# Window-attention scores on sixteen 32x32 tiles of the array, with their transposes in the shared ring of PSUM banks

## The chip, the cores and the metric
The kernel runs on one core of a Trainium2 chip. The time is what the device takes for one execution, in microseconds. "Before" is the median of three runs.

## What is computed
The input is x of shape (32, 256, 128). Four stages follow, each of the form x = x + f(layernorm(x)), cut here to what matters:

```python
# stage W: window attention, 16 heads of 8, keys and values shared by 8 heads each (KV = 2)
q = (x @ Wq + bq); k = (x @ Wk + bk); v = (x @ Wv + bv)      # 128, 16 and 16 columns
# blocks of 32 queries see 64 padded keys, u in [t, t + 32)
scores = where(win_mask, einsum('bhntd,bhnud->bhntu', qb, kb), -inf)
out = einsum('bhntu,bhnud->bhntd', softmax(scores), vb) @ Wo + bo
# stage F: h = x @ W_exp + b_exp; butterfly; gelu; butterfly; @ W_con + b_con
# stage L: linear attention, phi = elu + 1; out = q (k^T v) / (q sum(k)); @ Wproj + bproj
# stage G: the feed-forward stage again
```

## The kernel before, in words
The 8192 tokens are cut into 16 groups of 512 (four tiles of 128 tokens). A group passes through the stages P (norm, queries, keys, values), W (window attention), F (feed-forward), L (linear attention) and G (feed-forward again). The butterflies are folded at the start into two plain matrices, w1b and w2.

The kernel is a software pipeline written out by hand. Each engine runs its own list of work once per turn t (`turn`, one per engine), and each item works on group t - lag; the lags run from 0 to 6. The order of TensorE's items is the table PRODUCTS (lines 40 to 49): name, lag and PSUM bank. The lists of VectorE, ScalarE, GpSimdE and SyncE stand in their own `turn` functions and in VECTOR, PHI, POOL_STEPS, NORMED, BIASED and TRANSFERS. An engine works its list strictly in order. All waits are counts on semaphores: `product` counts finished products of TensorE, and `drained_b` counts how often bank b was emptied. `free(g, name)` (line 393) makes a product wait until the item before it on the same bank has been drained.

PSUM has eight banks of 512 fp32 columns. Before, ps_s has two (bank "S", the scores), ps_t has two (bank "T", the transposed scores), and four are the ring, "0" to "3", shared by 31 of the 39 products of a turn.

Names used below, with their lines: `P.kv` (508) and `P.q` (514) are the keys and values, and the queries. `W.S0` to `W.S3` (`scores`, 412) are the scores of tile j: first a bf16 product of the mask (422), then the fp32 product of queries and keys (427). `shift_by_max` (811) takes the row maximum and subtracts it (VectorE). `W.T0` to `W.T3` (438) are eight 128x128 transposes per tile; `probs_out` (674) takes the exp of them on ScalarE into probs_t. `W.PV0` to `W.PV3` (446) multiply with the values, `head_outputs` (823) divides by the sum. `W.V` (433) transposes the spread values. `W.oT`, `L.oT` and the four `.xT` (401) are four transposes each, copied out by ScalarE (`copy_out`, 659). `F.up0` to `F.up3`, `G.up0` to `G.up3` (461) are the up products, each followed by a gelu on ScalarE (665) into hid; `F.down`, `G.down` (468) use all four. `L.q`, `L.k0`, `L.k1`, `L.kv`, `L.out0`, `L.out1`, `L.proj` belong to linear attention. ScalarE alternates between exp and gelu, and each change of the function puts an ACT_TABLE_LOAD ahead of the ACTIVATE, at the ACTIVATE's line.

The scores need every head's keys in the partitions of its queries. `spread_keys` (283) copies the 8 rows of keys of each of the two key heads to the partitions of its eight query heads, one DMA per query head, sixteen a group, into a block-diagonal tensor kx, whose other entries are zero. A score matmul is then 64 rows (8 heads of 8) by 32 queries, with 8 heads x 64 keys = 512 columns; four blocks of 32 queries times two halves make eight matmuls on eight 64x32 tiles of the array.

```python
for c in range(4):
    for a in range(KV):
        half = slice(HPK * HD * a, HPK * HD * (a + 1))
        last = nc.tensor.matmul(
            ps_s[32 * c:32 * c + 32, a], q_t[half, P * j + 32 * c:P * j + 32 * c + 32],
            kx[half, :, TSPAN * j + 32 * c:TSPAN * j + 32 * c + SPAN], ...)
```

Of the kernel before, what the change touches and what calls it, by code (L numbers as in the profile page):

```python
# [7 lines left out]
F32 = mybir.dt.float32  # L8
BF16 = mybir.dt.bfloat16
# [8 lines left out]
WIN = 32  # L18
# [13 lines left out]
KVW = DIM + HEADS  # L32
LN_EPS = 1e-5
# [22 lines left out]
]  # L56
PHI = [("L.q", 3), ("L.k0", 3), ("L.k1", 3)]
POOL_STEPS = [
    ("L.rv", 5), ("L.rstd", 5), ("L.nm", 5), ("L.nmr", 5),
    ("F.rv", 3), ("F.rstd", 3), ("F.nm", 3), ("F.nmr", 3),  # L60
    ("W.rv", 2), ("W.rstd", 2), ("W.nm", 2), ("W.nmr", 2),
    ("P.rv", 0), ("P.rstd", 0), ("P.nm", 0), ("P.nmr", 0),
]
NORMED = [("L.xn", 5), ("F.xn", 3), ("W.xn", 2), ("P.xn", 0)]
BIASED = [("L.xb", 5), ("P.xb", 1), ("F.xb", 3), ("W.xb", 2)]
TRANSFERS = {"P.v": 2, "P.kx": 1, "P.x": 0, "G.y": 6}
TURNS = NG + 6
# [35 lines left out]
def window_and_linear_attention_with_butterfly_ffn(  # L103
    nc, x, wq, bq, wk, bk, wv, bv, wo, bo, wqkv_t, wproj_t, bproj, w_exp_t, up_m, up_c, up_b,
    down_m, down_c, w_con, b_con, down_b, ident_c, spread_c, kvmask_c, band_c, vones_c, out,
):
    with ExitStack() as ctx:
# [12 lines left out]
        bandb = sb("bandb", [P, HPK, SPAN], BF16)  # L120
        half = sb("half", [P, TILES])
        wq_s = sb("wq_s", [P, P])
        wkv_s = sb("wkv_s", [P, 2 * KV * HD])
# [4 lines left out]
        bkv_s = sb("bkv_s", [2 * KV * HD, 1])  # L128
# [31 lines left out]
        kv_t = sb("kv_t", [2 * KV * HD, TILES, TSPAN])  # L160
        kx = sb("kx", [P, HPK, TILES * TSPAN])
# [23 lines left out]
        ps_s = ctx.enter_context(nc.psum_tensor("ps_s", [P, 2, 512], F32))  # L185
        ps_t = ctx.enter_context(nc.psum_tensor("ps_t", [P, HPK, P], F32))
        ring = [ctx.enter_context(nc.psum_tensor(f"ring{i}", [P, 512], F32)) for i in range(4)]

        def bank(name):
# [23 lines left out]
                   for b in "ST0123"}  # L213
# [7 lines left out]
        kx_in = Count(sem("kx_in"), [("P.kx", TRANSFERS["P.kx"])], 16 * HEADS)  # L221
# [29 lines left out]
        def _(sp):  # L251
            consts = [(ident, ident_c), (spread, spread_c), (kvmask, kvmask_c), (band, band_c)]
            for dst, src in consts:
# [4 lines left out]
                (wq_s[:], wq), (wkv_s[:, 0:KV * HD], wk), (wkv_s[:, KV * HD:], wv), (bq_s[:], column(bq)),  # L258
                (bkv_s[0:KV * HD, :], column(bk)), (bkv_s[KV * HD:, :], column(bv)), (wo_s[:], wo),
# [35 lines left out]
            def spread_values(g):  # L295
# [4 lines left out]
                for c in range(4):  # L300
                    for kv in range(KV):
                        r = KV * HD + kv * HD
# [8 lines left out]
            def turn(t):  # L311
                for g in due(t, 2):
                    spread_values(g)
                for g in due(t, 1):
                    spread_keys(g)
                for g in due(t, 0):
                    load_x(g)
                for g in due(t, 6):
                    store_y(g)
# [7 lines left out]
        def _(pool):  # L327
# [41 lines left out]
            def turn(t):  # L369
                for g in due(t, 5):  # L370
                    normalise(g, "L")
                for g in due(t, 3):
                    normalise(g, "F")
# [6 lines left out]
                for g in due(t, 3):  # L380
                    add_bias(g, "F", bproj_s, "F.down", "L.proj")
                for g in due(t, 0):
                    normalise(g, "P")
                for g in due(t, 2):
                    add_bias(g, "W", bffn_s, "W.proj", "F.down")
# [6 lines left out]
        def _(pe):  # L392
# [19 lines left out]
            def scores(g, j):  # L412
# [623 lines left out]
```

## Time and profile before
| what | before |
|---|---|
| runs | 678.38, 679.83, 678.49 us; median 678.49 |
| profiled execution, own time | 678.38 us |
| span of the profile, first to last instruction | 676.6 us |
| instructions | 14602 |
| mean granted TensorE clock | 0.985 of 2.4 GHz |
| VectorE, ScalarE, GpSimdE busy | 419.6, 427.1, 308.8 us |

In rows of a timeline the first number is the start in us from the first instruction, the second the time until the last of the merged instructions ends, "x" their number. The ends of matmuls are modelled and overlap the next start, so the cost of a step is read from start to start. An fp32 matmul leaves two records. A bracket tells of idle time before a row, and who ended it.

### The profile page before, as it was taken

What the parts mean: (1) busy time and instruction counts of PE and PEld (TensorE: products, weight loads), DVE (VectorE), ACT (ScalarE), POOL (GpSimd) and SP (SyncE); (2) the same over time, 40 slices, a digit from 0 to 9 for tenths busy, and PEclk for the clock granted to TensorE, in tenths of its full rate; (3) what the DMA queues carried; (4) which work ended last, traced back from release to release, by engine and by line L of the source; (5) the groups of instructions that cost most, each with busy time, mean ns of one, the idle gap of its engine ahead of it and who ended that gap; (6) DMA issues with size and microseconds to landing.
All of it is one profiled execution on the core that took longest, in us unless ns stands there. A gap on an engine that the chain in (4) does not pass through costs nothing.

```text
span 676.6 us, 14602 instructions
## 1 busy us (share of the span) xinstructions
PE 623.5 (92%) x5140; PEld 409.5 (61%) x5140; DVE 419.6 (62%) x1114; ACT 427.1 (63%) x585; POOL 308.8 (46%) x585
## 2 busy tenths in 40 slices
PE   0847698999999999999999999999999999999986
PEld 0633354656575766757585757667575857575855
DVE  2356556677767666676667676666766676674340
ACT  0302275666868768685868687686858686868341
POOL 6002408164645354654546453546545464446332
PEclk9977899999999999999999999999999999999999
DMA  5500101101011110101111111101001111000001
GB/s 164 190 16 9 33 13 29 21 20 22 21 21 36 18 39 12 42 8 19 33 21 37 21 36 19 39 13 42 9 19 32 22 36 34 8 1 16 16 17 31
DMA packets 31671, 20.96 MB, mean 31 GB/s; under 512 B 9328, under 2 KB 27504, under 8 KB 31600
## 3 DMA queue, kind: packets, MB, share of 16 engines
q1 hardware_dynamic: 31600, 20.03, 12.1%
q8 instruction: 42, 0.69, 0.4%
q14 instruction: 29, 0.24, 0.1%
HBM read 9.53 MB, written 4.19 MB: 20 GB/s over the span
## 4 chain that ended last, share of the span: by engine, by line
PE 88%; DVE 5%; ACT 3%; issue 2%; SPq 1%; DMA 1%; POOL 0%; DVEq 0%; ACTq 0%
PE ring L475 18%; PE ring L465 17%; PE ps_t L443 8%; PE ring L403 8%; PE ps_s L427 8%; PE ring L452 5%; PE ring L484 4%; PE ring L500 4%; PE ps_s L422 3%; PE ring L508 2%; PE ring L535 2%; PE ring L524 2%; PE ring L514 2%; PE ring L491 2%; PE ps_t L562 1%
## 5 line engine op out<-in xcount | busy, mean ns | idle before, releaser
L814 DVE TENSOR_REDUCE rowmax<-ps_s 128x16 f32<-128x1024 f32 x64 | 78.0, 1219 | 39.6 <-PE ps_s L427 39.5
L679 ACT ACTIVATE probs_t<-ps_t 128x1024 f32<-128x1024 f32 x64 | 65.5, 1023 | 29.5 <-PE ps_t L443 29.0
L819 DVE TENSOR_TENSOR shifted<-ps_s,rowmax 128x1024 f32<-128x1024 f32 x64 | 78.4, 1225 | 7.0 <-PE ps_t L443 0.5
L671 ACT ACT_TABLE_LOAD x57 | 73.1, 1283 | 8.7 <-PE ring L465 7.9
L443 PE MATMUL ps_t<-ident,shifted 128*128 128x128 f32 x512 | 68.7, 278 | 3.3 <-DVE shifted L819 3.3
L679 ACT ACT_TABLE_LOAD x42 | 53.9, 1283 | 26.2 <-PE ps_t L443 26.2
L427 PE MATMUL ps_s<-kx,q_t 64*32 64x512 f32 x1024 | 70.2, 618 | 0.0
L465 PE MATMUL ring<-xT_G,w1b 128*128 128x512 f32 x128 | 67.4, 613 | 2.3 <-ACT xT_G L663 1.0
L443 PEld LDWEIGHTS ps_t<-ident,shifted 128*128 128x128 f32 x512 | 58.5, 143 | 12.6 <-issue 9.1
L475 PEld LDWEIGHTS ring<-w,hid_G 128*128 128x128 f32 x512 | 58.4, 192 | 9.5 <-issue 4.9
L475 PE MATMUL ring<-w,hid_G 128*128 128x128 f32 x512 | 61.2, 278 | 2.8 <-ACT hid_G L671 2.8
L475 PE MATMUL ring<-w,hid_F 128*128 128x128 f32 x512 | 60.9, 277 | 0.6 <-issue 0.2
L475 PEld LDWEIGHTS ring<-w,hid_F 128*128 128x128 f32 x512 | 58.4, 192 | 4.3 <-issue 4.3
L465 PE MATMUL ring<-xT_F,w1b 128*128 128x512 f32 x128 | 60.3, 595 | 0.4 <-ACT xT_F L663 0.4
L671 ACT ACTIVATE hid_G<-ring,b 128x512 f32<-128x512 f32 x64 | 43.9, 687 | 20.5 <-PE ring L465 20.0
L364 POOL TENSOR_TENSOR xb_P<-x_P,bo_s 128x512 f32<-128x512 f32 x16 | 20.5, 1282 | 73.5 <-DVE x_W L806 70.1
L338 POOL TENSOR_SCALAR rv_F<-mv_F 128x4 f32<-128x4 f32 x16 | 3.6, 226 | 96.5 <-DVE mv_F L792 96.5
L828 DVE STREAM_TRANSPOSE o_raw<-ring 128x256 f32<-128x256 f32 x64 | 28.2, 440 | 25.3 <-PE ring L452 25.2
L806 DVE TENSOR_TENSOR x_G<-ring,xb_L 128x512 f32<-128x512 f32 x16 | 11.1, 692 | 49.0 <-PE ring L475 49.0
L338 POOL TENSOR_SCALAR rv_L<-mv_L 128x4 f32<-128x4 f32 x16 | 3.6, 226 | 81.7 <-DVE mv_L L792 81.7
L671 ACT ACTIVATE hid_F<-ring,b 128x512 f32<-128x512 f32 x64 | 40.3, 688 | 0.4 <-PE ring L465 0.2
L452 PE MATMUL ring<-probs_t,vx 128*32 128x256 f32 x512 | 37.6, 388 | 0.0
(120 smaller groups left out, 1205.6 us busy)
## 6 DMA issues: line engine op xcount, KB each, us to landing
kx<-kv_t SPq DMA_DIRECT2D x256, 20.0 KB
x_P<-in_x SPq DMA_DIRECT2D x16, 256.0 KB, 2.9
out_x<-x_G SPq DMA_DIRECT2D x16, 256.0 KB, 3.2
vx_t<-kv_t SPq DMA_DIRECT2D x128, 8.0 KB
up_s<-in_up_m SPq DMA_DIRECT2D x7, 256.0 KB, 5.6
down_s<-in_down_m SPq DMA_DIRECT2D x7, 256.0 KB, 5.6
u_t<-in_w_exp_t SPq DMA_DIRECT2D x1, 258.0 KB, 3.7
vx_t<-in_vones_c SPq DMA_DIRECT2D x1, 256.0 KB, 2.9
```

Of the source, the lines that this page charges most:

```text
L403: last = nc.tensor.transpose(bank(name)[:, P * j:P * (j + 1)], src[:, j], ident[:])
L427: last = nc.tensor.matmul(ps_s[32 * c:32 * c + 32, a], q_t[half, P * j + 32 * c:P * j + 32 * c + 32], kx[half, :, TSPAN * j + 32 * c:TSPAN ...
L443: last = nc.tensor.transpose(ps_t[:, h], shifted[:, j % 2, h].rearrange("p k u -> p (k u)"), ident[:])
L452: last = nc.tensor.matmul(bank(name)[32 * c:32 * c + 32, 0:HPK * 32], vx[:, j, c], probs_t[:, j % 2, :, 32 * c:32 * c + 32], start=True, s ...
L465: nc.tensor.matmul(bank(name)[:], w1b[:, P * c:P * (c + 1)], x_t[s][:], start=True, stop=True).then_inc(product.sem, 1)
L475: last = nc.tensor.matmul(bank(name)[:, P * j:P * (j + 1)], hid[s][:, c, P * j:P * (j + 1)], w2[:, c], start=(c == 0), stop=(c == CH - 1))
L484: last = nc.tensor.matmul(bank(f"{s}.proj")[:, P * j:P * (j + 1)], src[:, P * j:P * (j + 1)], weights[:], start=True, stop=True)
L671: nc.scalar.activation(hid[s][:, c], bank(name)[:], ACT.Gelu, bias=b1[:, c:c + 1]).then_inc(drained[BANK[name]].sem, 1)
L679: nc.scalar.activation(probs_t[:, j % 2], ps_t[:], ACT.Exp).then_inc(drained["T"].sem, 1)
L814: nc.vector.tensor_reduce(rowmax[:, j], s, AX_X, ALU.max).then_inc(vec.sem, 1)
L819: nc.vector.tensor_tensor(shifted[:, j % 2].rearrange("p h k u -> p k h u"), ps_s[:].rearrange("p k (h u) -> p k h u", u=SPAN), m, ALU.sub ...
L828: nc.vector.transpose(o_raw[:, j % 2].rearrange("p h r -> p (h r)"), bank(name)[:, 0:HPK * 32]).then_inc(own.sem, 1)
```

## The change
The scores run on sixteen 32x32 tiles: a matmul has 32 rows (4 heads of 8), 32 queries and 4 heads x 64 keys = 256 columns; row strip r writes the first 256 columns of bank r of ps_s, which now has four banks. The order of the query columns is changed on the host (`query_order`), so that a strip holds heads of both key heads in turn. The weights of the keys are repeated four times (`key_rows`), so that P.kv gives 64 rows of keys and 16 of values, and `spread_keys` needs four DMAs of 32 rows each instead of sixteen of 8. ps_t is gone: the eight transposes of a tile are two products, W.Tja and W.Tjb, of four transposes each, in banks of the ring, and each half is drained by its own exp. At the start, the butterflies' down product uses a bank of ps_s. All lists have a new order, lags and banks; TensorE's lags now run from 0 to 5, and the scores of tiles 0 and 1 are made in the turn of their keys.

```diff
 PRODUCTS = [
+    ("W.S2", 1, "S"), ("G.up2", 5, "3"), ("G.up0", 5, "1"), ("W.PV0", 1, "0"), ("F.xT", 2, "2"),
+    ("W.T1b", 1, "3"), ("L.k1", 3, "1"), ("L.k0", 3, "0"), ("W.PV1", 1, "3"), ("F.up2", 2, "2"),
+    ("W.S3", 1, "S"), ("P.xT", 0, "1"), ("F.up1", 2, "3"), ("F.up0", 2, "0"), ("G.up1", 5, "2"),
+    ("L.kv", 3, "1"), ("W.T2b", 1, "2"), ("P.kv", 0, "3"), ("W.T2a", 1, "0"), ("W.T3a", 1, "1"),
+    ("W.T3b", 1, "2"), ("L.out1", 3, "3"), ("W.PV2", 1, "0"), ("F.up3", 2, "1"), ("W.PV3", 1, "2"),
+    ("P.q", 0, "3"), ("F.down", 2, "1"), ("L.out0", 3, "0"), ("W.S0", 0, "S"), ("W.oT", 1, "3"),
+    ("G.down", 5, "2"), ("G.xT", 4, "3"), ("W.proj", 1, "1"), ("L.oT", 3, "0"), ("G.up3", 4, "2"),
+    ("W.S1", 0, "S"), ("L.xT", 2, "0"), ("W.T0b", 0, "1"), ("W.T0a", 0, "3"), ("L.q", 2, "2"),
+    ("L.proj", 3, "0"), ("W.V", 0, "3"), ("W.T1a", 0, "1"),
 ]
...
-                for h in range(HEADS):
-                    kv = h // HPK
-                    sp.dma_start(kx[h * HD:(h + 1) * HD, h % HPK],
-                                 kv_t[kv * HD:(kv + 1) * HD].rearrange("d j n -> d (j n)")).then_inc(kx_in.sem, 16)
+                for h in range(RH):
+                    kv = h % KV
+                    sp.dma_start(kx[h:P:RH, h], kv_t[kv * ROWS * HD:(kv + 1) * ROWS * HD].rearrange("d j n -> d (j n)")
+                                 ).then_inc(kx_in.sem, 16)
...
-                    for a in range(KV):
-                        half = slice(HPK * HD * a, HPK * HD * (a + 1))
+                    for r in range(ROWS):
+                        rows = slice(32 * r, 32 * r + 32)
                         last = nc.tensor.matmul(
-                            ps_s[32 * c:32 * c + 32, a], q_t[half, P * j + 32 * c:P * j + 32 * c + 32],
-                            kx[half, :, TSPAN * j + 32 * c:TSPAN * j + 32 * c + SPAN],
+                            ps_s[32 * c:32 * c + 32, r, 0:RH * SPAN], q_t[rows, P * j + 32 * c:P * j + 32 * c + 32],
+                            kx[rows, :, TSPAN * j + 32 * c:TSPAN * j + 32 * c + SPAN],
...
-            def probs_transposed(g, j):
+            def probs_transposed(g, j, part):
-                for h in range(HPK):
-                    last = nc.tensor.transpose(ps_t[:, h], shifted[:, j % 2, h].rearrange("p k u -> p (k u)"), ident[:])
+                for i, h in enumerate(PAIRS[part]):
+                    last = nc.tensor.transpose(bank(name)[:, P * i:P * (i + 1)],
+                                               shifted[:, j % 2, h].rearrange("p k u -> p (k u)"), ident[:])
...
-                nc.scalar.activation(probs_t[:, j % 2], ps_t[:], ACT.Exp).then_inc(drained["T"].sem, 1)
+                nc.scalar.activation(probs_t[:, j % 2, PAIRS[part][0]:PAIRS[part][-1] + 1].rearrange("p h t -> p (h t)"),
+                                     bank(name)[:], ACT.Exp).then_inc(drained[BANK[name]].sem, 1)
```

ScalarE's new list per turn, lags in brackets: copy L.xT (3), exp T0a and T0b (1), phi of L.q (3), exp T1a (1), gelu G2 and G0 (5), exp T1b (1), copy F.xT (2), phi and copies of L.k1 and L.k0 (3), gelu F2 (2), copy P.xT (0), gelu F1 and F0 (2), gelu G1 (5), exp T2b (1), drain P.kv (0), exp T2a, T3a and T3b (1), gelu F3 (2), drain P.q (0), copies of W.oT (1), G.xT (4) and L.oT (3), gelu G3 (4). The lists of VectorE, GpSimdE and SyncE are reordered in the same way. The groups of a turn of ScalarE and of TensorE may be numbered with lags that differ by one where the work crosses the end of a turn.

## Rows read from the trace of the kernel before

**Rows 1.** The page, part 1: busy time, share of the span and instructions.
```profile
PE 623.5 (92%) x5140; PEld 409.5 (61%) x5140; DVE 419.6 (62%) x1114; ACT 427.1 (63%) x585; POOL 308.8 (46%) x585
```

**Rows 2.** Timeline of TensorE, P.kv of groups 1, 4, 8 and 15.
```profile
59.92 1.04 PE L508 MATMUL ring<-xT_P,wkv_s 128*32 128x512 f32 x2
...
153.05 1.04 PE L508 MATMUL ring<-xT_P,wkv_s 128*32 128x512 f32 x2
...
298.08 1.04 PE L508 MATMUL ring<-xT_P,wkv_s 128*32 128x512 f32 x2
...
558.25 1.04 PE L508 MATMUL ring<-xT_P,wkv_s 128*32 128x512 f32 x2
```

**Rows 3.** Timeline of TensorE inside one full turn.
```profile
308.54 3.84 PE L475 MATMUL ring<-w,hid_G 128*128 128x128 f32 x32
312.21 1.02 PE L514 MATMUL ring<-xT_P,wq_s 128*128 128x512 f32 x2
313.17 0.64 PE L452 MATMUL ring<-probs_t,vx 128*32 128x256 f32 x8
313.74 0.76 PE L535 MATMUL ring<-kvs,phi_q 128*128 128x144 f32 x4
314.33 0.60 PE L403 MATMUL ring<-ident,xn_L 128*128 128x128 f32 x4
314.77 0.66 PE L535 MATMUL ring<-kvs,phi_q 128*128 128x144 f32 x4
...
316.71 1.06 PE L484 MATMUL ring<-wo_s,o_wt 128*128 128x128 f32 x8
...
334.68 0.60 PE L403 MATMUL ring<-ident,vx_t 128*128 128x128 f32 x4
335.21 1.04 PE L508 MATMUL ring<-xT_P,wkv_s 128*32 128x512 f32 x2
336.19 0.41 PE L422 MATMUL ps_s<-bandb,spreadb 64*32 64x512 bf16 x8
336.41 1.04 PE L427 MATMUL ps_s<-kx,q_t 64*32 64x512 f32 x16
337.38 1.07 PE L452 MATMUL ring<-probs_t,vx 128*32 128x256 f32 x16
```

**Rows 4.** Timeline of ScalarE inside the same turn.
```profile
315.96 0.60 ACT L663 ACTIVATE o_wt<-ring 128x512 f32<-128x512 f32 x1 [0.33 <-PE ring L403]
...
318.25 0.69 ACT L671 ACTIVATE hid_G<-ring,b 128x512 f32<-128x512 f32 x1
318.83 0.59 ACT L663 ACTIVATE xT_L<-ring 128x512 f32<-128x512 f32 x1
319.31 0.60 ACT L663 ACTIVATE o_lt<-ring 128x512 f32<-128x512 f32 x1
...
324.29 0.36 ACT L698 ACTIVATE v_ext<-ring 128x256 f32<-128x256 f32 x1
...
325.29 0.37 ACT L698 ACTIVATE v_ext<-ring 128x256 f32<-128x256 f32 x1
...
333.20 1.28 ACT L679 ACT_TABLE_LOAD   x1 [0.26 <-PE ps_t L443]
334.50 1.02 ACT L679 ACTIVATE probs_t<-ps_t 128x1024 f32<-128x1024 f32 x1
...
336.37 0.87 ACT L708 ACTIVATE kv_t<-ring,bkv_s 32x288 f32<-32x288 f32 x2 [0.85 <-PE ring L508]
...
338.56 0.69 ACT L671 ACTIVATE hid_F<-ring,b 128x512 f32<-128x512 f32 x1
```

**Rows 5.** The page, part 5, groups: busy, mean ns of one, idle before.
```profile
L814 DVE TENSOR_REDUCE rowmax<-ps_s 128x16 f32<-128x1024 f32 x64 | 78.0, 1219 | 39.6 <-PE ps_s L427 39.5
...
L679 ACT ACT_TABLE_LOAD x42 | 53.9, 1283 | 26.2 <-PE ps_t L443 26.2
```

**Rows 6.** Timeline of SyncE's queue: four of the sixteen key transfers.
```profile
337.63 2.69 SPq L292 DMA_DIRECT2D kx<-kv_t  x4
```

More of the change, by code:

```diff
@@ L32 @@
 KVW = DIM + HEADS
+ROWS = 4
+RH = HEADS // ROWS
+KROWS = KV * ROWS * HD
+KVROWS = KROWS + KV * HD
 LN_EPS = 1e-5
@@ L369, in turn @@
             def turn(t):
-                for g in due(t, 5):
-                    normalise(g, "L")
+                for g in due(t, 4):
+                    add_bias(g, "F", bproj_s, "F.down", "L.proj")
                 for g in due(t, 3):
+                    add_bias(g, "W", bffn_s, "W.proj", "F.down")
                     normalise(g, "F")
@@ L507, in attention_kv @@
                 free(g, "P.kv")
-                nc.tensor.matmul(bank("P.kv")[0:2 * KV * HD, :], wkv_s[:], x_t["P"][:], start=True, stop=True
+                nc.tensor.matmul(bank("P.kv")[0:KVROWS, :], wkv_s[:], x_t["P"][:], start=True, stop=True
                                  ).then_inc(product.sem, 1)
@@ L561, in butterflies @@
                     for c in range(CH):
-                        last = nc.tensor.matmul(ps_t[:, c], down_s[m][:, c], d_t[n % 2][:, c],
+                        last = nc.tensor.matmul(ps_s[:, 2, P * c:P * (c + 1)], down_s[m][:, c], d_t[n % 2][:, c],
                                                 start=True, stop=True)
@@ L573, in turn @@
             def turn(t):
-                for g in due(t, 2):
+                for g in due(t, 1):
+                    scores(g, 2)
+                for g in due(t, 5):
+                    ffn_up(g, "G", 2)
+                    ffn_up(g, "G", 0)
+                for g in due(t, 1):
+                    weighted_values(g, 0)
+                for g in due(t, 2):
+                    norm_transposed(g, "F", "W")
+                for g in due(t, 1):
+                    probs_transposed(g, 1, "b")
+                for g in due(t, 3):
+                    linear_kv_rows(g, 1)
+                    linear_kv_rows(g, 0)
+                for g in due(t, 1):
+                    weighted_values(g, 1)
+                for g in due(t, 2):
+                    ffn_up(g, "F", 2)
+                for g in due(t, 1):
+                    scores(g, 3)
+                for g in due(t, 0):
+                    norm_transposed(g, "P", "P")
+                for g in due(t, 2):
+                    ffn_up(g, "F", 1)
+                    ffn_up(g, "F", 0)
+                for g in due(t, 5):
+                    ffn_up(g, "G", 1)
+                for g in due(t, 3):
+                    linear_state(g)
+                for g in due(t, 1):
+                    probs_transposed(g, 2, "b")
+                for g in due(t, 0):
+                    attention_kv(g)
+                for g in due(t, 1):
+                    probs_transposed(g, 2, "a")
+                    probs_transposed(g, 3, "a")
+                    probs_transposed(g, 3, "b")
+                for g in due(t, 3):
+                    linear_out(g, 1)
+                for g in due(t, 1):
                     weighted_values(g, 2)
-                for g in due(t, 6):
-                    ffn_down(g, "G")
+                for g in due(t, 2):
+                    ffn_up(g, "F", 3)
                 for g in due(t, 1):
+                    weighted_values(g, 3)
+                for g in due(t, 0):
                     attention_q(g)
@@ L582, in turn @@
                 for g in due(t, 2):
-                    weighted_values(g, 3)
-                for g in due(t, 4):
+                    ffn_down(g, "F")
+                for g in due(t, 3):
                     linear_out(g, 0)
-                for g in due(t, 5):
-                    norm_transposed(g, "G", "L")
-                for g in due(t, 4):
-                    linear_out(g, 1)
-                for g in due(t, 2):
+                for g in due(t, 0):
+                    scores(g, 0)
@@ L637, in turn @@
[L637 to L647 removed]
+                    norm_transposed(g, "L", "F")
+                for g in due(t, 0):
+                    probs_transposed(g, 0, "b")
+                    probs_transposed(g, 0, "a")
@@ L903, in turn @@
             def turn(t):
+                for g in due(t, 3):
+                    residual(g, "F", "F.down", "W")
+                    moments(g, "F")
                 for g in due(t, 4):
-                    linear_normalised(g, 1)
+                    linear_normalised(g, 0)
+                for g in due(t, 1):
+                    shift_by_max(g, 0)
+                for g in due(t, 6):
+                    residual(g, "G", "G.down", "L")
                 for g in due(t, 2):
@@ L919, in turn @@
                         butterflies()
+                for g in due(t, 1):
+                    head_outputs(g, 0)
+                    shift_by_max(g, 2)
                 for g in due(t, 3):
```

270 lines of the change are left out of this document (118 added, 152 removed), and 16 rows, old and new, of tables (PRODUCTS, VECTOR).

## The prediction
> **What bounds the kernel now.** First I read the page's busy times: TensorE is busy 623.5 of 676.6 us [rows 1]. The starts of one product that occurs once a turn, the keys and values of a group (P.kv), then give the rhythm [rows 2]: 59.92 for group 1, 153.05 for group 4, 298.08 for group 8 and 558.25 for group 15. With the next start, 335.21 [rows 3], a full turn is 37.13 us, and a turn of the filling pipeline about 31. The timeline of TensorE inside a turn shows step after step without an idle bracket [rows 3], so the bound is TensorE's own list of work. The timeline of ScalarE shows something else [rows 4]: the load of an activation table (1.28 us) begins only after the product that its ACTIVATE waits for is done; the row at 333.20 has 0.26 us of idle time before it, ended by PE, and the group of these loads has 26.2 us of idle time, all ended by the transposes [rows 5]. Today this delay holds nobody up: the transposes have ps_t for themselves and return to it a quarter of a turn later.
>
> **What the change does to TensorE's work.** Steps are distances between starts. Four transposes take 0.44 (314.33 to 314.77), a 512-column product 0.96 less 0.09 = 0.87, PV 0.57, a down product 3.67, two state products with the entry into another array shape 0.59 [rows 3]. That entry costs 0.09: the values' transposes take 0.53 where 32-column work follows, 0.44 elsewhere.
> Scores: the masks take 0.22 (336.19 to 336.41), the scores 0.97 (to 337.38), together 1.19 per tile, four per turn [rows 3]. The eight matmuls of 64x32 run side by side, for 0.22 is one 512-column pass. Sixteen 32x32 ones of 256 columns would halve the passes (0.11 + 0.43) if they ran side by side too. The way out of the shape (0.11, 1.19 less 0.22 and 0.86) stays, and sixteen instead of eight weight loads must fit under shorter passes, for which I add 0.1. So 0.75. No row shows a 32x32 tile; the bounds are 0.65 (all overlapped) and 1.19 (no gain), and nothing excludes more than 1.19. I take a value near the low end, since half as many columns per tile is the same kind of work as the row before.
> In a sentence by itself: the Trainium skill, TensorE: Matmul & The Clock Gate, section "Wait — 56ns, not 53.3ns?", states a floor of about 25 ns between the starts of matmuls however narrow, and by it 48 of them would take 1.2 us and the gain would be nil; whether that holds across separate tiles, the rows of this kernel decide (rival B).
> The rest of the work: PV0 and PV1 lose their neighbourhood with a score step, which adds two entries and 0.1 of exit (+0.3); P.kv widens from 32 to 80 columns and so is no longer a narrow tile (-0.1). TensorE's work per turn goes from 37.1 to 37.1 - 4x0.44 + 0.2 = 35.6; adding up the steps of the new order gives 35.0; I take 35.3.
>
> **What it adds: waits for banks.** The transposes of the probabilities now come in eight halves and take turns with everything else on four ring banks: 39 products a turn in place of 31. Who must drain a bank before the next product starts is read off the new list. Where that drain begins with a table load, the way from the end of a product to the next start on its bank is: 0.30 until ScalarE starts (P.kv ends at 335.21 + 0.87, its drain starts at 336.37), 1.30 for the load (333.20 to 334.50), the ACTIVATE, and 0.15 back (o_wt ends at 316.56, the product that needs it starts at 316.71) [rows 3, 4]. A half's exp has no row; a copy of the same 512 columns takes 0.60, and between two that follow each other 0.48; gelu takes 0.69, or 0.58 in a row; the three steps of k 1.00 per half; kv's two 0.87 [rows 4]. The two halves cost ScalarE about what the whole did (0.48 + 0.60 against 1.02). The new order has six loads in a turn, the old one eight.
> Going once around a full turn, from the start of the values' transposes (V):
> 1. V to end of G.up2: T1a waits for the exp of T0b (0.48), then T1a 0.44 + 0.09, S2 0.75, G.up2 0.87: 2.63.
> 2. G.up2 to T1b (bank 3): 0.30 + 1.30 + 0.69 + 0.15 = 2.44. TensorE has 1.97 of work to put there. Then T1b 0.44.
> 3. T1b to T2b: ScalarE without a gap does load, exp, copy of F.xT, k1, k0, load, gelu F2, copy of P.xT, F1, F0, G1: 0.30+1.30+0.48+0.48+2.00+0.10+1.30+0.58+0.48+0.58+0.58+0.69+0.15 = 9.02; TensorE has 8.1 there. Then T2b 0.44.
> 4. T2b to PV2 (T2b's exp, kv's drain, T2a's exp): 0.30+1.30+0.48+0.87+0.60+0.15 = 3.70 against 2.8. Then PV2 0.57 and F.up3 0.87.
> 5. F.up3 to F.down: 2.44 against 1.5.
> 6. F.down to the end of T0a, TensorE alone: 3.67+0.59+0.75 (S0)+0.44+3.67+0.44+0.87+0.44+0.96+0.75 (S1)+0.44+0.88 = 13.90.
> 7. T0a to V (bank 3): 0.30+1.30+0.60+0.15 = 2.35 against 1.7.
> Sum 2.63+2.44+0.44+9.02+0.44+3.70+1.44+2.44+13.90+2.35 = **38.8 us**, against 37.13 now. S3 lies in stretch 3, under ScalarE, so its gain is worth nothing; three score steps count. With 0.65 for them the loop is 38.5, with 1.19 it is 40.1.
> On the loads trace and skill differ: here one costs 1.30 with what lies around it [rows 4]. The Trainium skill, ScalarE: Activation LUTs, section "What ACT_TABLE_LOAD costs", gives 1283 ns and adds a drain of some 1380 ns; by that the five loads of the loop would add 6.9 us to it. The trace has the 1.28 and not the drain.
> Other engines: VectorE's reductions and subtractions keep 1024 elements a partition, 1.22 us each [rows 5]; S2 to S3 leave it more than 7 us for 2.5. GpSimdE's list only changes its order. SyncE issues four key transfers a group in place of sixteen, at 0.67 each (2.69 for four) [rows 6]. In full turns nobody waits for keys: P.kv to S0 leaves 9 us. If a transfer four times as large landed later by as much, S0 would wait; I count nothing and keep up to 1 us a turn for the range.
>
> **The sum.** Up to P.kv of group 1 nothing changes (59.9). The three turns from there to group 4 take 93.1 now; they are bound by latency, of which twelve issues of 0.67 = 8 us go, fully in the first and less as work fills the turns, and fewer table loads are in them. Between 69 and 93 I take 80. Then one turn without the down product of G, 38.8 - 3.7 = 35, and ten full turns, 388: P.kv of group 15 at 563. From there to the end it is 118.3 now; the last group has the same stages before it, at five lags instead of six, and the chains of each stage (moments, normalising, transposing, gelu) stay; between 113 and 125 I take 120. Span 683, with the 1.8 us that lie around the span in the profiled execution (678.38 against 676.6) 685. The profiled execution is 0.1 us under the median of the three, 678.49.
>
> **Rivals.**
> A, *TensorE stays the bound.* If the table loads ran while TensorE still worked on the product (or the waits overlapped otherwise), stretches 2 to 5 and 7 shrink below TensorE's work and a turn is 35.3: 59.9 + 80 + 32 + 353 + 118 + 1.8 = 645. For it: TensorE has no idle bracket in a full turn today [rows 3]. Against it: every load on the timeline comes after its product. It decides once the waits sum to under 1.8 us a turn; by the walk they sum to 3.8. Chance 0.16.
> A', *half of it*: chains shorter by 0.2 to 0.3 each, a turn of 36 to 37.8, 655 to 677. Chance 0.16.
> B, *the sixteen tiles don't run together*: the score step stays at 1.19, a turn is 40.1 and the fill a little longer: 685 + 11x1.3 + 2 = 701. Chance 0.10.
> C, *keys late*: one wait of 1 us per turn at S0: 696. Chance 0.06.
>
> **The numbers.** The forecast, the loop of 38 to 39.6, has 0.52: 677 to 694. Most of it is slower; 0.2% (1.4 us) is what a measurement of this kernel can tell. Faster: A, A' less a little, and some of the forecast, 0.31. Same 0.07. Slower 0.62. The range leaves out most of A and the far side of B: 656 to 703.
>
> **What would show it.** P.kv to P.kv in the full turns near 38.8; TensorE's busy share down to about 90% there; waits of F.down on hid_F near 0.9, of T1b on hid_G 0.5, of V on probs_t 0.6 and of T2b on hid_G, each once a turn; the score step 0.75, the sixteen masks starting together; six loads a turn; 0.44 for each half's transposes. The forecast is wrong if TensorE has no waits in the full turns (A), or if the score step is above 1 us (B).

## The result and the profile after

| | before | after |
|---|---|---|
| median of the runs (4 each, same chip) | 679.16 us (678.38 to 680.63) | 726.85 us (723.81 to 727.71) |
| span of the profile | 676.6 us | 722.0 us |
| P.kv of group 1 starts at | 59.9 | 63.4 |
| P.kv 1 to P.kv 4 | 93.1 | 92.1 |
| P.kv 4 to P.kv 15 | 405.2 | 434.9 |
| P.kv 15 to the end | 118.3 | 131.6 |
| one full turn | 37.13 | 39.73 |
| table loads in the whole run | 114 | 92 |

The ratio is 1.069, with a 95% interval of 1.065 to 1.073. The kernel became slower, as forecast, but by 48 us and not by 6.5, and 726.85 is above the upper end of the range (703). The two profiled executions differ by 45.4 us of span: 29.7 us of it, two thirds, lie between P.kv 4 and P.kv 15, in the full turns, and 13.3 us behind the last P.kv.

First the page of the changed kernel: busy times [rows 1], chain of waits by engine, and the groups that answer to [rows 5].

```profile
PE 632.7 (88%) x6676; PEld 423.5 (59%) x6676; DVE 420.1 (58%) x1114; ACT 398.8 (55%) x627; POOL 305.8 (42%) x585
...
PE 72%; ACT 12%; DVE 8%; issue 6%; SPq 1%; DMA 1%; POOL 0%; ACTq 0%; DVEq 0%; POOLq 0%
...
L832 DVE TENSOR_REDUCE rowmax<-ps_s 128x16 f32<-128x1024 f32 x64 | 77.9, 1217 | 7.2 <-PE ps_s L429 6.3
L682 ACT ACT_TABLE_LOAD x46 | 59.0, 1283 | 34.3 <-PE ring L469 34.0
...
L690 ACT ACT_TABLE_LOAD x41 | 52.6, 1283 | 19.3 <-PE ring L445 19.3
```

ScalarE is less busy than before (398.8 against 427.1 us): 22 loads of 1.28 us are gone, which is 28.2 of these 28.3. TensorE's share of the span falls from 92 to 88%, and its share of the chain that ended last from 88% (the same line of the page before) to 72%. The load groups say where to look: 34.0 us of idle time ahead of gelu's loads end with an up product, 19.3 us ahead of exp's loads with a transpose. The reduction costs what it did (1217 ns), so VectorE's own work isn't the matter.

TensorE's P.kv of groups 1, 4 and 15, which answer to [rows 2]:

```profile
63.40 1.08 PE L512 MATMUL ring<-xT_P,wkv_s 128*80 128x512 f32 x2
...
155.49 1.02 PE L512 MATMUL ring<-xT_P,wkv_s 128*80 128x512 f32 x2
...
590.40 1.02 PE L512 MATMUL ring<-xT_P,wkv_s 128*80 128x512 f32 x2
```

TensorE's timeline in one full turn (answers to [rows 3]; first the start, then the time until the last of the merged instructions ends):

```profile
311.68 0.63 PE L445 MATMUL ring<-ident,shifted 128*128 128x128 f32 x4
312.14 1.02 PE L512 MATMUL ring<-xT_P,wkv_s 128*80 128x512 f32 x2
313.00 1.04 PE L445 MATMUL ring<-ident,shifted 128*128 128x128 f32 x8
314.42 0.63 PE L445 MATMUL ring<-ident,shifted 128*128 128x128 f32 x4 [0.39 <-ACT probs_t L690]
...
315.86 0.64 PE L456 MATMUL ring<-probs_t,vx 128*32 128x256 f32 x8
316.42 1.13 PE L469 MATMUL ring<-xT_F,w1b 128*128 128x512 f32 x2
...
318.05 1.13 PE L518 MATMUL ring<-xT_P,wq_s 128*128 128x512 f32 x2
319.86 3.81 PE L479 MATMUL ring<-w,hid_F 128*128 128x128 f32 x32 [0.69 <-DVE o_raw L846]
...
336.45 0.63 PE L405 MATMUL ring<-ident,vx_t 128*128 128x128 f32 x4 [0.23 <-ACT probs_t L690]
...
337.50 0.33 PE L424 MATMUL ps_s<-bandb,spreadb 32*32 32x256 bf16 x16
337.62 0.91 PE L429 MATMUL ps_s<-kx,q_t 32*32 32x256 f32 x32
338.47 1.98 PE L469 MATMUL ring<-xT_G,w1b 128*128 128x512 f32 x4
...
341.80 0.63 PE L445 MATMUL ring<-ident,shifted 128*128 128x128 f32 x4 [0.20 <-ACT hid_G L682]
342.38 1.97 PE L504 MATMUL ring<-wl_s,xT_L 128*128 128x256 f32 x8
344.75 0.64 PE L456 MATMUL ring<-probs_t,vx 128*32 128x256 f32 x8 [0.41 <-ACT probs_t L690]
...
351.50 0.63 PE L445 MATMUL ring<-ident,shifted 128*128 128x128 f32 x4
```

Before, this view had no bracket in a full turn. Now there are five, all for drains that ScalarE does, together 1.92 us. The one of F.down at 319.86 names VectorE's o_raw, but F.down neither reads o_raw nor writes the bank that it empties. What it needs in the kernel are the gelus of the four up products, and the last of them, that of F.up3, also empties F.down's own bank. ScalarE's timeline shows it (it answers to [rows 4]):

```profile
317.63 1.28 ACT L682 ACT_TABLE_LOAD   x1 [1.13 <-PE ring L469]
318.93 0.69 ACT L682 ACTIVATE hid_F<-ring,b 128x512 f32<-128x512 f32 x1
...
334.42 1.28 ACT L690 ACT_TABLE_LOAD   x1 [0.26 <-PE ring L445]
335.71 1.09 ACT L690 ACTIVATE probs_t<-ring 128x512 f32<-128x512 f32 x2
...
339.67 1.28 ACT L682 ACT_TABLE_LOAD   x1 [1.24 <-PE ring L469]
...
342.51 1.28 ACT L690 ACT_TABLE_LOAD   x1 [0.28 <-PE ring L445]
```

F.up3 starts at 316.42 and ScalarE waits for it; only when it is done does the load begin (317.63), then the gelu (318.93 to 319.62), then F.down (319.86). ScalarE had stood idle for 1.13 us, in which most of the load would have fitted. This is the loop that the prediction walked.

### The profile page after: what moved, and what is told of

Its sections match the earlier page's. It is cut to its first block, busy times and chain, and to the rows that moved or that the text cites. A ratio compares the mean times of both kernels' runs of the same rounds, so it can differ in the third digit from the quotient of the medians.

```text
span 722.0 us, 17701 instructions
## 1 busy us (share of the span) xinstructions
PE 632.7 (88%) x6676; PEld 423.5 (59%) x6676; DVE 420.1 (58%) x1114; ACT 398.8 (55%) x627; POOL 305.8 (42%) x585
## 4 chain that ended last, share of the span: by engine, by line
PE 72%; ACT 12%; DVE 8%; issue 6%; SPq 1%; DMA 1%; POOL 0%; ACTq 0%; DVEq 0%; POOLq 0%
PE ring L479 16%; PE ring L469 14%; PE ring L405 7%; PE ring L445 7%; PE ps_s L429 6%; PE ring L456 4%; ACT probs_t L690 3%; PE ring L504 3%; PE ring L539 3%; PE ring L495 2%; PE ps_s L424 2%; ACT L682 2%; PE ring L512 2%; PE ring L528 2%; ACT hid_G L682 2%
## 5 line engine op out<-in xcount | busy, mean ns | idle before, releaser
L445 PE MATMUL ring<-ident,shifted 128*128 128x128 f32 x512 | 74.6, 280 | 10.6 <-ACT probs_t L690 7.2
L690 ACT ACTIVATE probs_t<-ring 128x512 f32<-128x512 f32 x128 | 70.7, 596 | 21.9 <-PE ring L445 21.4
L832 DVE TENSOR_REDUCE rowmax<-ps_s 128x16 f32<-128x1024 f32 x64 | 77.9, 1217 | 7.2 <-PE ps_s L429 6.3
L445 PEld LDWEIGHTS ring<-ident,shifted 128*128 128x128 f32 x512 | 58.1, 144 | 29.9 <-issue 25.5
L469 PE MATMUL ring<-xT_F,w1b 128*128 128x512 f32 x128 | 66.7, 624 | 0.1
L469 PE MATMUL ring<-xT_G,w1b 128*128 128x512 f32 x128 | 64.9, 613 | 1.8 <-ACT xT_G L674 1.4
L690 ACT ACT_TABLE_LOAD x41 | 52.6, 1283 | 19.3 <-PE ring L445 19.3
L479 PE MATMUL ring<-w,hid_G 128*128 128x128 f32 x512 | 59.9, 275 | 1.9 <-ACT hid_G L682 1.9
L429 PE MATMUL ps_s<-kx,q_t 32*32 32x256 f32 x2048 | 60.4, 394 | 0.0
L674 ACT ACTIVATE o_wt<-ring 128x512 f32<-128x512 f32 x16 | 9.6, 597 | 85.0 <-PE ring L405 85.0
L456 PE MATMUL ring<-probs_t,vx 128*32 128x256 f32 x512 | 40.9, 390 | 7.2 <-ACT probs_t L690 7.2
L682 ACT ACTIVATE hid_F<-ring,b 128x512 f32<-128x512 f32 x64 | 42.4, 690 | 3.8 <-PE ring L469 3.3
L824 DVE TENSOR_TENSOR x_F<-ring,xb_W 128x512 f32<-128x512 f32 x16 | 11.1, 692 | 56.1 <-PE ring L479 56.1
```

The lines of the kernel that those rows point to most:

```text
L429: last = nc.tensor.matmul(ps_s[32 * c:32 * c + 32, r, 0:RH * SPAN], q_t[rows, P * j + 32 * c:P * j + 32 * c + 32], kx[rows, :, TSPAN * j + ...
L445: last = nc.tensor.transpose(bank(name)[:, P * i:P * (i + 1)], shifted[:, j % 2, h].rearrange("p k u -> p (k u)"), ident[:])
L456: last = nc.tensor.matmul(bank(name)[32 * c:32 * c + 32, 0:HPK * 32], vx[:, j, c], probs_t[:, j % 2, :, 32 * c:32 * c + 32], start=True, s ...
L469: nc.tensor.matmul(bank(name)[:], w1b[:, P * c:P * (c + 1)], x_t[s][:], start=True, stop=True).then_inc(product.sem, 1)
L479: last = nc.tensor.matmul(bank(name)[:, P * j:P * (j + 1)], hid[s][:, c, P * j:P * (j + 1)], w2[:, c], start=(c == 0), stop=(c == CH - 1))
L682: nc.scalar.activation(hid[s][:, c], bank(name)[:], ACT.Gelu, bias=b1[:, c:c + 1]).then_inc(drained[BANK[name]].sem, 1)
```

## The experiments

**1. Are the waits the table loads?** Gelu is replaced by exp in both feed-forward stages, so that ScalarE never changes its table; what these stages compute is thus another function, of the same sizes, and a 512-column drain costs ScalarE 0.69 us with either. The same edit went into the kernel before.

```diff
-  nc.scalar.activation(hid[s][:, c], bank(name)[:], ACT.Gelu, bias=b1[:, c:c + 1]
+  nc.scalar.activation(hid[s][:, c], bank(name)[:], ACT.Exp, bias=b1[:, c:c + 1]
```

> The changed kernel with exp in place of gelu in both feed-forward stages, so that the function computed there is another one and ScalarE never changes its table. Theory L (the banks of the ring wait behind table loads): the 87 loads go, a full turn falls from 39.73 to TensorE's own work, 36.2 to 36.6 us, and the span from 722 to 670-685. Rival R (the ring is too full whatever the drains begin with): a turn stays above 38.5 us and the span above 705.

> The kernel before with the same replacement of gelu by exp. Both theories: a full turn is TensorE's work already, 37.13, and loses at most the 0.25 us wait of F.down: 36.8 to 37.1. Filling and draining lose a few loads on their chains: span 664 to 673. If a full turn falls by more than 0.5 us, loads were on the path of the old kernel too and the account of the change is wrong.

Measured, one execution each: the changed kernel 670.01 us, a full turn 36.49, from P.kv 15 to the end 118.3; the kernel before 671.19 us, 36.87 and 116.0. One load is left in each. So 91 loads less are worth 53.8 us of span in the changed kernel (722.0 to 668.2) and 113 less only 7.2 us in the one before (676.6 to 669.4). The price of a load is its place, not its number. And with the loads gone the changed kernel isn't slower: its turn is shorter by 0.38 us.

**2. The same functions, the loads earlier.** Exp alone proves too much (it takes the loads away, not their delay). So at six changes of the function a one-column ACTIVATE of the coming function on constant data stands ahead of the instruction that waits; the diff shows the one at F.up3. All loads and all of the computation stay.

```diff
+ def touch(func):
+     n = len(touched)
+     touched.append(func)
+     nc.scalar.activation(scratch[:, n:n + 1], bq_s[:], func)
...
  for g in due(t, 2):
+     touch(ACT.Gelu)
      gelu(g, "F", 3)
```

> The changed kernel; ScalarE gets a one-column ACTIVATE of the coming function ahead of the wait at each of the six changes of table in a turn, so that the load runs before the product is done; nothing else. Theory L: each wait behind a load shortens by up to 1.3 us where ScalarE is idle before it; full turn 36.3 to 37.0, time 675 to 692. Rival R: turn within 0.5 us of 39.73, time above 720.

> The kernel before with the same one-column ACTIVATEs ahead of its eight changes of table a turn. Full turns are TensorE's work: 36.9 to 37.15 us. Filling and draining have chains with loads on them (waits of 0.93 us of G.down on the last gelu): time 665 to 676 against 679. If the small ACTIVATEs themselves get in the way, 679 to 685.

Measured: the changed kernel 687.01 us, ratio to the kernel before 1.011 (1.010 to 1.013), with the same 92 loads and a turn of 36.96. The kernel before with the edit (eight changes a turn) 681.1 us, ratio 1.002 (1.001 to 1.003), turn 37.22. That is a little above what was expected: there was nothing to hide, and the small ACTIVATEs (0.20 us each) probably stand in the way, which no run shows apart. ScalarE's and TensorE's timelines of the changed kernel with early loads, at F.up3 and F.down:

```profile
302.18 1.28 ACT L747 ACT_TABLE_LOAD   x1
303.48 0.20 ACT L747 ACTIVATE scratch<-bq_s 128x1 f32<-128x1 f32 x1
303.59 0.67 ACT L683 ACTIVATE hid_F<-ring,b 128x512 f32<-128x512 f32 x1
```

```profile
302.08 1.12 PE L470 MATMUL ring<-xT_F,w1b 128*128 128x512 f32 x2
303.14 0.64 PE L457 MATMUL ring<-probs_t,vx 128*32 128x256 f32 x8
303.71 1.13 PE L519 MATMUL ring<-xT_P,wq_s 128*128 128x512 f32 x2
304.67 3.73 PE L480 MATMUL ring<-w,hid_F 128*128 128x128 f32 x32
```

The load now runs beside F.up3 (302.18 against 302.08), and F.down has no bracket. From start to start, both kernels: PV2 to F.down 4.00 before the edit and 3.15 with it, T2b to PV2 4.18 and 3.43, T1b to T2b 9.70 and 9.02, V to T1b 5.35 and 4.98, F.down to V 16.59 and 16.37. These five differences add up to 2.87 us, which is the difference of the two turns that were read (39.82 against 36.95). **The waits in the turn are the loads that begin only behind the product.**

**3. The score step.** It was predicted at 0.75 us and is 0.963 (337.50 to 338.47 in the timeline above): the masks 0.12, as expected, the scores 0.844 where 0.64 was counted. Looking at the score product in ever longer windows from its start shows how its 32 records begin:

```profile
337.62 0.40 PE L429 MATMUL ps_s<-kx,q_t 32*32 32x256 f32 x8
...
337.62 0.70 PE L429 MATMUL ps_s<-kx,q_t 32*32 32x256 f32 x24
```

Eight start before 337.70, sixteen more before 337.95, the last eight after that: three waves, where two full passes of sixteen would have done. Is that due to the order, in which the four strips of a block follow each other? The two loops were exchanged.

```diff
-  for c in range(4):
-      for r in range(ROWS):
-          rows = slice(32 * r, 32 * r + 32)
+  for r in range(ROWS):
+      rows = slice(32 * r, 32 * r + 32)
+      for c in range(4):
```

> The changed kernel with the sixteen masks and the sixteen score matmuls of a tile issued row strip by row strip instead of column block by column block; same work. In the changed kernel the 32 score records start in three waves (8, 16, 8) and the step is 0.96 us with the mask. Theory W (only eight weight loads run ahead, whatever their place): three waves again, 0.96. Theory S (weights for a strip whose matmuls are running have to wait, so strips should alternate late): two waves, step 0.75, a full turn 0.6 us shorter, span 715.

Measured, one execution: 725.21 us, turn 39.73, masks 0.12, scores 0.84 as before. The order of the tiles has no part in it. Why it is three waves (whether, say, no more than eight weights are loaded ahead) stays open; no run tested it further.

**4. What the narrower tiles and the four key transfers are worth.** The changed kernel got the scores of the kernel before back (eight 64x32 tiles of 512 columns), first with sixteen key transfers.

```diff
-  for r in range(ROWS):
-      rows = slice(32 * r, 32 * r + 32)
+  for r in range(2):
+      rows = slice(64 * r, 64 * r + 64)
...
-  for h in range(RH):
+  for r in range(ROWS):
+      for h in range(RH):
```

> The changed kernel with the score matmuls back on eight 64x32 tiles over two PSUM banks and the keys spread by sixteen transfers; order, halves and the four-bank ring are the changed kernel's. It prices the 32x32 tiles alone: the score step goes back from 0.96 to 1.20, three of the four count, so a full turn is 40.4 (39.73 + 0.7) and the span 732. Rival (the waits of ScalarE absorb all of it): 39.7 to 39.9, 724.

Measured, one execution: 821.47 us and a turn of some 46. That was no measure of the tiles. SyncE, TensorE and the windows around S0:

```profile
362.88 11.07 SPq L297 DMA_DIRECT2D kx<-kv_t  x16
```

```profile
375.43 0.63 PE L425 MATMUL ps_s<-bandb,spreadb 64*32 64x512 bf16 x8 [3.46 <-issue]
375.81 1.95 PE L430 MATMUL ps_s<-kx,q_t 64*32 64x512 f32 x16
377.69 1.11 PE L406 MATMUL ring<-ident,o_w 128*128 128x128 f32 x4
```

In the windows the columns are length, busy time of PE, PEld, DVE, ACT and POOL, granted clock, DMA share, GB/s.

```profile
371.90:375.40 3.50, 0.07 (x1) 0.00 (x1) 2.51 (x12) 0.00 (x0) 1.44 (x3) 0.83 0.17 29
375.40:381.00 5.60, 5.57 (x40) 3.76 (x41) 2.45 (x2) 0.60 (x1) 2.00 (x6) 0.50 0.09 16
```

Sixteen issues take 11 us, S0 of the same turn waits 3.46 us for the last keys, and the granted clock is 0.83 over this wait and 0.50 (its 1.2 GHz level) in the 5.6 us behind it, where masks and scores together take 2.26 us (375.43 to 377.69) in place of 1.20. So the repeated keys, which looked like a side matter of this change, are what allows S0 to stand in the turn of its keys. With another order of the query columns, eight transfers of 16 rows serve the 64x32 tiles:

```diff
+  for h in range(HPK):
+      row0 = (h % KV) * ROWS * HD
+      sp.dma_start(kx[h:P:HPK, h], kv_t[row0:row0 + 2 * HD].rearrange("d j n -> d (j n)")
```

> The 64x32 run again, with another order of the query columns so that eight transfers of 16 rows spread the keys instead of sixteen of 8. The issues end 5.4 us after the first instead of 10.7, S0 starts 9 us after it in the changed kernel, so it waits no more. What is left is the price of the tile: full turn 40.4 (39.73 + 3x0.235), span 728 to 735. If the turn stays near 46, it was not the keys that held S0.

Measured, one execution: 747.31 us, turn 40.66, score step 1.20:

```profile
380.05 0.41 PE L424 MATMUL ps_s<-bandb,spreadb 64*32 64x512 bf16 x8
380.28 1.04 PE L429 MATMUL ps_s<-kx,q_t 64*32 64x512 f32 x16
381.25 0.66 PE L405 MATMUL ring<-ident,o_w 128*128 128x128 f32 x4
```

The turn is longer by 0.93 and four steps by 4 x 0.235 = 0.94: all four steps count, S3 too. The time is above what was expected (span 745.5): P.kv 1 came 5.1 us later than with the narrow tiles, and P.kv 1 to P.kv 4 took 6.7 us more, of which one wait of S0 for keys is 3.2. So in this list the narrow tiles bring 0.93 us a turn, and eight transfers with wide tiles cost 23.5 us of span against four with narrow ones. The number of transfers shows in the filling: from P.kv 1 to P.kv 2 it takes 35.95 us with sixteen and 30.8 with eight (granted clock 0.81 and 0.80), and 24.1 with four and the narrow tiles (1.00).

In the kernel before, the same eight transfers alone:

```diff
-  for h in range(HEADS):
-      kv = h // HPK
-      sp.dma_start(kx[h * HD:(h + 1) * HD, h % HPK],
-                   kv_t[kv * HD:(kv + 1) * HD].rearrange("d j n -> d (j n)")).then_inc(kx_in.sem, 16)
+  for h in range(HPK):
+      sp.dma_start(kx[h:P:HPK, h], kv_t[0:KV * HD].rearrange("d j n -> d (j n)")
+                   ).then_inc(kx_in.sem, 16)
```

> The kernel before with its query columns reordered so that eight transfers of 16 rows spread the keys, nothing else: one part of the change alone. In full turns the keys land a quarter of a turn early in any case: 37.13 us, no change. In the first turns S0 waits for the last keys by 0.3 to 0.7 us. Time 676 to 679.5 against 679.6; if SyncE's queue set the length of the filling turns (31 us each), they shorten by up to 5 us each: 665 to 670.

Measured: 679.65 us, ratio 1.0003 (0.9993 to 1.0013), turn 37.13. In the old list the issues are hidden, and all but hidden in the filling too: with sixteen transfers S0 of group 1 waits 0.44 us for its last keys.

```profile
75.05 0.41 PE L422 MATMUL ps_s<-bandb,spreadb 64*32 64x512 bf16 x8 [0.44 <-issue]
```

With eight that wait is gone, and from P.kv 1 to P.kv 2 it still took 33.4 us for 31.1, at a granted clock of 0.85 for 0.95.

**5. Banks of their own for the transposed halves.** With 64x32 scores, ps_s needs two banks, and the a halves and the b halves can have one each outside the ring, first with sixteen key transfers, without and with early loads.

```diff
-    ("W.T1b", 1, "3"), ... ("W.T2b", 1, "2"), ("W.T2a", 1, "0"), ("W.T3a", 1, "1"),
+    ("W.T1b", 1, "5"), ... ("W.T2b", 1, "5"), ("W.T2a", 1, "4"), ("W.T3a", 1, "4"),
```

> As the run with 64x32 score tiles, and the transposed halves have two banks of their own (a and b), so that nobody but the next transpose waits for their exp; the order is the changed kernel's. Theory L: V no longer waits for T0a nor T1b for G.up2, but PV1 still waits for its own exp (0.5), PV2 (0.9) and F.down (0.9) for a function behind a load: full turn 38.9 to 39.6, that is 0.8 to 1.5 under the 64x32 run. If sharing the ring is all of the cost: 37.4 or less.

> The run before with the one-column ACTIVATEs ahead of the table changes. Both causes are gone, TensorE's own work is left: 36.5 (measured without tables) + 4x0.235 (score step) = 37.4 to 37.6 us a turn, time 690 to 698. It must come out above the changed kernel with early loads (687.0), by the price of the 64x32 tiles; if it comes out below, the halves in the ring cost something beside the loads.

Measured: 796.01 us, ratio 1.171 (1.169 to 1.173), and 786.39 us, 1.156 (1.153 to 1.159), with turns of 42 to 46. Late keys are in both (S0 waits 29.4 and 47.9 us for them in all), so they say nothing of the banks. Both again with eight transfers:

> The run with banks of their own for the transposed halves, with eight key transfers. Theory L as before: the ring waits of V and T1b go, those for data behind a load stay: full turn 38.9 to 39.8. If sharing the ring is all of the cost: 37.5 or less. If it changes nothing against the 64x32 run with eight transfers: 40.4.

> The same with the one-column ACTIVATEs ahead of the table changes: TensorE's own work with 64x32 tiles, 37.4 to 37.6 us a turn, time 690 to 698.

Measured, one execution each: 758.02 us with a turn of 41.11, and with early loads 720.56 us with 38.89. Both missed: banks of their own made the turn longer by 0.45 than the ring (40.66, experiment 4), not shorter. TensorE with own banks, T3a:

```profile
376.29 1.06 PE L445 MATMUL ring<-ident,shifted 128*128 128x128 f32 x8 [2.08 <-ACT probs_t L690]
```

T2a and T3a follow each other on one bank, so T3a waits 2.1 us until T2a's exp is done. In the ring T2a, T3a and T3b lie on three different banks. From start to start against the ring with the same tiles and transfers: T2b to PV2 5.46 us for 4.17, but V to T1b 5.14 for 5.58 and F.down to V 16.67 for 17.06. So the waits of V and T1b for a shared bank did go (0.83 us), and the two halves of neighbouring tiles on one bank cost 1.29 us. F.down's wait stays at 0.69, since it is for data. With early loads the wait of T3a, 1.47 us, is the only bracket of the turn; without it 38.89 would be 37.4, as was expected. The run replaces one sharing by another; it doesn't show what banks without any sharing would bring.

**6. The tail.** With the early loads 127.5 us are still left behind P.kv 15, against 118.3 without any. In the last turns groups are missing from ScalarE's list, and a function then meets another neighbour. Three more one-column ACTIVATEs, only in turns in which the group of lag 1 or 2 is missing:

```diff
+     if not due(t, 1):
+         touch(ACT.Exp)       # at two places
...
+     if not due(t, 2):
+         touch(ACT.Gelu)
```

> The changed kernel with early loads (687.0), and in the last turns, where the exps of the window attention are gone, three more one-column ACTIVATEs: exp ahead of L.q and L.k1, gelu ahead of G1. Theory L for the tail (131.6 us after P.kv of group 15, 127.5 with early loads, 118.3 without tables): the two loads that follow a relu on the chain of the two turns without lag 1 or 2 go, 4 x 1.28 = 5 us less: tail 122.5, time 682. Rival (the tail is long because of the order and its dependences): tail 127, time 687.

Measured: 683.74 us, ratio 1.007 (1.005 to 1.009), turn 36.95, tail 123.9, where 122.5 was expected. TensorE in the last turns, the linear stage's k products of group 15, in the changed kernel, with the early loads of experiment 2, and in this run:

```profile
686.53 2.71 PE L504 MATMUL ring<-wl_s,xT_L 128*128 128x256 f32 x8 [2.75 <-ACT hid_G L682]
```

```profile
648.56 3.75 PE L505 MATMUL ring<-wl_s,xT_L 128*128 128x256 f32 x8 [2.84 <-ACT hid_G L683]
```

```profile
645.16 1.97 PE L505 MATMUL ring<-wl_s,xT_L 128*128 128x256 f32 x8 [1.69 <-ACT hid_G L683]
```

The wait is 1.15 us shorter than with the early loads alone. The same products also run faster: from their start to the next product's it is 3.55 us with the early loads of experiment 2 (granted clock 0.79 from 645 to 650 and 0.52 from 650 to 655), 2.50 in the changed kernel and 1.80 here, at full clock. So the 3.6 us that the tail lost are not loads alone: its time at the 1.2 GHz level fell from 6.8 to 3.4 us, which is up to 1.7 us (an estimate: half of the difference).

**7. PV and scores side by side.** The prediction charged 0.3 us a turn for entries between array shapes. On top of experiment 6, PV0 was put right behind S2 and S3 right behind PV1, where no wide product lies between.

```diff
-    ("W.S2", 1, "S"), ("G.up2", 5, "3"), ("G.up0", 5, "1"), ("W.PV0", 1, "0"), ("F.xT", 2, "2"),
+    ("W.S2", 1, "S"), ("W.PV0", 1, "0"), ("G.up2", 5, "3"), ("G.up0", 5, "1"), ("F.xT", 2, "2"),
...
-    ("W.PV1", 1, "3"), ("F.up2", 2, "2"), ("W.S3", 1, "S"),
+    ("W.PV1", 1, "3"), ("W.S3", 1, "S"), ("F.up2", 2, "2"),
```

> The run before, with two of TensorE's steps moved: PV0 right behind S2 and S3 right behind PV1. Each move joins two pieces of tiled work, which saves one entry of 0.09 us; ScalarE's and VectorE's lists stay. A full turn 36.96 - 0.2 = 36.8, time 2 us under the run before (680). If F.up2, which comes 0.96 us later, delays its gelu, a turn grows by 0.3 to 0.6 us instead.

Measured: 689.58 us, ratio 1.016 (1.013 to 1.018), turn 37.24. A miss: 0.29 longer, not shorter. TensorE and ScalarE in the stretch that was rearranged:

```profile
328.63 0.64 PE L457 MATMUL ring<-probs_t,vx 128*32 128x256 f32 x8
329.20 1.98 PE L470 MATMUL ring<-xT_G,w1b 128*128 128x512 f32 x4
331.02 0.60 PE L406 MATMUL ring<-ident,xn_W 128*128 128x128 f32 x4
```

```profile
330.42 0.69 ACT L681 ACTIVATE hid_G<-ring,b 128x512 f32<-128x512 f32 x1 [0.31 <-PE ring L470]
331.28 0.69 ACT L681 ACTIVATE hid_G<-ring,b 128x512 f32<-128x512 f32 x1 [0.17 <-PE ring L470]
```

The entries were saved as the prediction had priced them: the pair G.up2, G.up0 takes 1.82 for 1.91 from start to start, F.up2 0.96 for 1.06, and the transposes behind either lose 0.06 and 0.05, together 0.30. But G.up2 and G.up0 stand 0.57 later (PV0 is ahead of them), and ScalarE now waits for each. Their gelus empty the banks of T1b and L.k1, and T1b's exp, which PV1 needs, comes behind them in ScalarE's list: from T1b to PV1 it takes 2.77 for 2.26 us. The list has no slack there in which to shift them. No version run here that computes the same function is faster than the kernel before; of the changed one, experiment 6 has the best time.

## Why the prediction was right or wrong

**Direction, and the mechanism in the full turns: right.** In a turn TensorE now stands in the chain product, table load, ACTIVATE, and then the next product on that bank or the one that reads the data (experiment 2). It waits at V (0.23), T1b (0.20) and F.down (0.69), as the text said, though each wait is shorter than given (0.6, 0.5, 0.9). Part of that is the bracket, which leaves out what the modelled ends cover: taken from start to start against experiment 1 the three are 0.39, 0.35 and 0.84. The rest is that TensorE's own steps between are longer. The wait at T2b didn't come; PV1 (0.41) and T3b (0.39) wait instead, and of PV1 the text didn't speak. Rivals A and A' fell. Experiment 1 bounds what A could have given: with no load in the way TensorE's list takes 36.49, not 35.3. 0.85 of these 1.2 us are the score steps; the rest isn't assigned. C did not occur: with four transfers no key was late in a full turn, for the last is issued at 317.54 and S0 starts at 324.10; experiment 4 shows the wait with sixteen.

**The seven stretches.** Measured against forecast: (1) 2.98 for 2.63, (2) 2.37 for 2.44, (3) 9.26 for 9.02, (4) 3.72 for 3.70, (5) 2.38 for 2.44, (6) 14.35 for 13.90, (7) 2.24 for 2.35. The four around a table load (2, 4, 5, 7) sum to 10.71 for 10.93. The three with a score step were all too short.

**The mis-sized terms, in the sum.** What failed is the size of four terms of the sum; 39 us of span are missing from it.
- "So 0.75", with "three score steps count": +11.9 us from P.kv 4 to P.kv 15 (434.9 for 423; 2.4 of them in the turn without G.down, 37.39 for 35). The step is 0.963. Three of them are 0.64 a turn, in stretches 1 and 6. The fourth, S3, was said to lie "under ScalarE"; that failed too. In stretch 3 PV1 waits for T1b's exp, and from its start (344.75) TensorE works without a bracket to T2b (351.50), S3 among it; ScalarE has a gap there. The load that counts is exp's ahead of PV1, and the rest is TensorE's list. Experiment 4 shows all four steps counting.
- "Between 69 and 93 I take 80": 92.1, at the far end. Its premise was that twelve issues, 8 us, stand on the path. In the old list they don't: S0 waited 0.44 us for the keys of the first of these turns (experiment 4). That turn is shorter all the same (24.1 us for 31.1), in a list that has S0 earlier; how much of that is the order was not told apart. The next two gave 6.0 back (34.5 and 33.5 for 30.2 and 31.8). Without loads the three take 85.7 (experiment 1), so 6.4 us of this error go with the loads; the granted clock from P.kv 2 to P.kv 4 is 0.97 with them and 1.00 without. The other 5.7 were not told apart. With and without loads S1 waits 1.3 us for VectorE in the second and in the third of these turns.
- "I take 120": 131.6. Without loads it is 118.3, so 13.3 us go with the loads, where all loads of the kernel before cost its tail 2.3 us (experiment 1). The text kept the chains of each stage and forgot that the loads now stand in them. Not all of the 13.3 is the loads' own time: behind two of the waits the granted clock falls (0.69 from 655 to 660 us, 0.76 from 685 to 690), which it doesn't do in this part of the run without loads. There 6.8 us pass at the 1.2 GHz level, up to 3.4 us of loss (an estimate: half of it).
- "Up to P.kv of group 1 nothing changes": +3.5 us. The row to see is S3 of group 0:

```profile
60.02 0.44 PE L424 MATMUL ps_s<-bandb,spreadb 32*32 32x256 bf16 x16 [1.55 <-DVE shifted L838]
```

In the new list four score products lie ahead of P.kv of group 1, in the old one three (it started at 59.92 [rows 2], with S3 behind it). S3 waits until VectorE has emptied ps_s, and P.kv waits behind S3. Experiment 1 has the delay as well (65.1 for 61.2), so loads are not its cause. No run took S3 from ahead of P.kv, so this is read from the timelines only.

Together 11.9 + 12.1 + 11.6 + 3.5 = 39.1 us. Three of the four lie before or after the full turns, and the prediction gave each a sentence or two where the turn had seven walked stretches.

**The two rules.** Rival B had the step at 1.19. It is 0.963, so the tiles do overlap, but B was nearer than it looked. The Trainium skill, TensorE: Matmul & The Clock Gate, section "Wait — 56ns, not 53.3ns?", has a floor of about 25 ns between matmul starts; by it, as an estimate, sixteen masks would take 0.4 us and the trace shows 0.12, so it does not hold across separate tiles here. For the 32 score records it would give 0.80, close to the 0.844 measured, but eight of them start within 0.08 us (experiment 3), so it isn't that floor that sets them either. The whole step, 0.96, lies between the rule's 1.2 and the 0.75 that was taken. The second, that of a drain of 1380 ns around a load (the Trainium skill, ScalarE: Activation LUTs, section "What ACT_TABLE_LOAD costs"), is not borne out: load start to ACTIVATE start is 1.30 us in the rows above. The prediction counted five loads in the loop there; its own stretches have six, so by that rule the loop would have been 8.3 us longer and not 6.9. The measured turn is 0.9 us over the 38.8.

## What to carry to other kernels

Where two functions of ScalarE alternate, ask of each table load which wait stands ahead of its ACTIVATE, not how many loads there are: the same 92 loads cost 54 us of span in one place and 17 us when six of a turn stand a few instructions earlier. A buffer that is shared can turn an engine's hidden delay into a wait of the next user, so when banks are pooled, walk the loop drain by drain, and put a one-column ACTIVATE of the coming function ahead of the wait. Work out fill and tail by the same walk as the steady turn: they held 27 of the 39 us that were missing here.

## What the runs showed that was not expected

- Sixteen 32x32 tiles take 0.844 us for fp32 scores of 256 columns, where eight 64x32 tiles take 0.97 for 512: half the columns save 13%. The bf16 masks did halve, from 0.22 to 0.12.
- SyncE's time per key transfer hardly depends on its size: 0.69 us for 8 rows (11.07 for sixteen), 0.62 for 16 (4.97 for eight), and for 32 rows:

```profile
315.08 2.46 SPq L296 DMA_DIRECT2D kx<-kv_t  x4
```

  which is 0.62. In this range the number of transfers counts, not the rows of each.
- Behind a wait of 3.46 us at S0 the granted clock stood at 0.50 for 5.6 us (experiment 4), which costs some 2.8 us on top of the wait (an estimate: half of the stretch, for TensorE is busy in nearly all of it).
